# A mixture-of-experts layer on one core: the second lowest pick's rows come in by an adding DMA, the third lowest pick's during the loop, and the first products no longer stand behind the slot lists

## The reference, cut to what matters

```python
def _L0_ffn_ref(h, gate_w, gu_w, dp_w, sh_gate_w, sh_up_w, sh_down_w, sh_gate1_w):
    ...
    logits = x @ gate_w.T
    topv, topi = jax.lax.top_k(logits, TOP_K)
    rw = jax.nn.softmax(topv.astype(jnp.float32), axis=-1).astype(x.dtype)
    W = jnp.zeros((N, E), x.dtype).at[jnp.arange(N)[:, None], topi].set(rw)
    gu = jnp.einsum('nh,eih->nei', x, gu_w)
    gate, up = (gu[..., :I], gu[..., I:])
    inter = jax.nn.silu(gate) * up
    inter_w = inter * W[:, :, None]
    out = jnp.einsum('nei,ehi->nh', inter_w, dp_w)
    ...
    out = out + sh_g * sh_out
    return out.reshape(Bb, Tt, Hh)
x = L0_attn_X
...
h = _layernorm(x, axis=-1) * (1 + ca) + sa
x = x + ga * _L0_attn_ref(h, L0_attn_W_in, L0_attn_b_in, L0_attn_W_out, L0_attn_b_out)
h = _layernorm(x, axis=-1) * (1 + cb) + sb
x = x + gb * _L0_ffn_ref(h, L0_ffn_gate_w, ...)
return x
```

## Time and profile before

| | us |
|---|---|
| median of 3 runs (981.03 to 982.82) | 981.03 |
| the profiled execution's own time | 980.68 |
| its span, first to last instruction | 978.9 |
| the first two tiles' products | 378.7 to 389.0 |
| loop at its steady pace | 402.5 to about 897 |
| last result tile copied on DVE | 902.9 |
| first late read issued after the loop | 906.2 |
| last DVE step of the last group | 976.4 |

### The profile page before, as it was taken

How to read it: one execution, slowest core, us unless ns; L and a number is a source line. 1 busy time by engine, 2 the same in 40 slices (tenths; PEclk the granted TensorE clock), 3 DMA queues, 4 the chain that set the end, 5 groups by cost and what they waited for, 6 DMA issues and landing times.

```text
span 978.9 us, 18595 instructions
## 1 busy us (share of the span) xinstructions
PE 918.3 (94%) x3569; PEld 565.5 (58%) x3570; DVE 551.1 (56%) x1466; ACT 270.7 (28%) x789; POOL 465.7 (48%) x462
## 2 busy tenths in 40 slices
PE   6999999999999796799999999999999999997796
PEld 2434534444453543677777777777777777775342
DVE  3685776678767752344444444444444444444897
ACT  2012313123210301233333333333333333332000
POOL 0000035406615677466666657666656666666000
PEclk9999999999999699799999999999999999999799
DMA  9914003012102143477666778777778767897798
GB/s 341 327 69 151 1 0 102 1 44 76 28 0 69 46 146 92 154 237 245 232 232 229 257 250 278 271 242 241 237 234 274 248 235 235 297 400 287 278 420 341
DMA packets 68518, 192.06 MB, mean 196 GB/s; under 512 B 19926, under 2 KB 20438, under 8 KB 68104
## 3 DMA queue, kind: packets, MB, share of 16 engines
q1 hardware_dynamic: 38232, 120.28, 34.4%
q0 software_dynamic: 30256, 71.43, 22.2%
HBM read 158.98 MB, written 52.54 MB: 216 GB/s over the span
## 4 chain that ended last, share of the span: by engine, by line
PE 64%; DMA 8%; DVE 7%; POOL 6%; issue 6%; SPq 1%; DVEq 0%; POOLq 0%
PE bank L1612 25%; PE bank L1620 13%; PE bank L1385 7%; PE bank L1607 6%; POOL slot_table L566 5%; PE bank L1430 4%; DMA wqkv<-in_experts 3%; PE bank L1396 3%; DMA front<-y_rows 2%; PE bank L1627 2%; PE bank L1685 1%; DMA slot_table<-pair,place 1%; PE bank L1407 1%; DMA y_rows<-front,sid 1%; PE bank L1494 1%
## 5 line engine op out<-in xcount | busy, mean ns | idle before, releaser
L1612 PE MATMUL bank<-wqkv,h2T 128*128 x1280 | 306.2, 382 | 0.8 <-DMA wqkv<-in_experts 0.8
L566 POOL DMA_INDIRECT slot_table<-pair,place x128 | 129.7, 1013 | 250.2 <-DVE place L1003 187.5
L1612 PEld LDWEIGHTS bank<-wqkv,h2T 128*128 128x128 f32 x1280 | 232.9, 192 | 26.8 <-issue 1.3
L614 POOL DMA_INDIRECT y_rows<-front,sid x160 | 163.4, 1021 | 130.0 <-issue 68.4
L604 POOL DMA_INDIRECT front<-h_rows,gid x167 | 170.9, 1023 | 58.5 <-issue 44.0
L1620 PE MATMUL bank<-wqkv,front 128*128 x320 | 164.5, 596 | 1.4 <-DVE front L1290 1.4
L795 ACT ACTIVATE h2T<-bank 128x512 f32<-128x512 f32 x162 | 96.6, 597 | 202.5 <-PE bank L1607 202.5
L1290 DVE COPY front<-bank 128x128 f32<-128x128 f32 x160 | 46.7, 292 | 168.4 <-PE bank L1627 165.9
L1284 DVE COPY front<-bank 128x512 f32<-128x512 f32 x160 | 110.7, 692 | 43.3 <-PE bank L1620 43.0
L1607 PEld LDWEIGHTS bank<-const,front 128*128 128x128 f32 x648 | 81.2, 142 | 90.0 <-issue 85.3
L1385 PE MATMUL bank<-wqkv,front 128*128 128x512 f32 x256 | 115.6, 603 | 8.3 <-DVEq L935 6.2
(11 more groups left out here) (237 smaller groups left out, 757.7 us busy)
## 6 DMA issues: line engine op xcount, KB each, us to landing
wqkv<-in_experts SPq DMA_DIRECT2D x64, 768.0 KB
front<-y_rows SPq DMA_DIRECT2D x20, 768.0 KB, 9.5
wqkv<-y_rows SPq DMA_DIRECT2D x12, 768.0 KB, 13.1
front<-in_w_mod SPq DMA_DIRECT2D x5, 1024.0 KB, 10.2
x<-in_x SPq DMA_DIRECT2D x4, 1024.0 KB, 11.1
h_rows<-h SPq DMA_DIRECT2D x4, 1024.0 KB, 4.6
out_dram<-x SPq DMA_DIRECT2D x16, 256.0 KB, 10.2
wqkv<-in_w_in SPq DMA_DIRECT2D x3, 1024.0 KB, 13.7
```

The costliest lines, as they stand in the source:

```text
L566: pool.indirect_dma_start(out=slots[:, :], out_offset=bass.IndirectOffsetOnAxis(ap=place[b % 2][:, i, k:k + 1], axis=0), in_=pair[:, b * T ...
L614: pool.indirect_dma_start(out=y_rows[:, :], out_offset=bass.IndirectOffsetOnAxis(ap=sid[:, s:s + 1], axis=0), in_=yb[s % YBUFS], in_offset ...
L1612: mm = pe.matmul(bank[2 + s % 2][:, 0:GU], xT[s % 4][:, k, :], wqkv[:, bass.ds(w + k * GU, GU)], start=(k == 0), stop=(k == KC - 1))
```

## The change

Three things change.

1. **Products ahead of lists.** In the first round DVE no longer makes the lists of tiles 5, 6 and 7 (and waits for all table parts) before its first product. `gated(0)` is its first step; the lists of tiles 5 to 14 are made in later steps as the table `LISTS` says, one or two per step. The wait for table parts 3 to 5 now stands in step 3, ahead of the list of tile 7.
2. **Early and late picks.** Pick 7 is still read in the loop; in place of pick 6, pick 5 is (`read_early(2, 1, ...)`, which waits for expert 59 to have landed). Pick 6 is not read by SP at all: when POOL has issued everything of the loop, it issues 16 DMAs of 256 KB that add pick 6's rows onto pick 7's in `early[0]` (`accum_op=ALU.add`). They count up four semaphores `s_acc`, one for each four groups. DVE's 16 additions of L1317 go, and its second step of group g waits for the four additions of g's batch.
3. **Six groups of five late rows.** Five picks are read late: 0 to 2 (768 KB) and 3 to 4 (512 KB) by the two `read_back` of a group. There are six buffers (`BACK = 6`) in place of five, so the reads of group g+6 are issued when group g is finished. DVE's first step of a group adds pick 5 (`early[1]`) to pick 4.

```diff
--- before.py
+++ after.py
@@ -54,8 +54,10 @@
 ROUNDS = EXPERT_TILES // ROUND
 assert AHEAD <= ROUND == PLAN - EXPERT_TILES
 DUMMY_COL = EV * SLOT_COLS
-BACK = 5
-EARLY = 2
+BACK = 6
+EARLY = 3
+EARLY_ROWS = 2
+LOW = 3
 LATE = TOPK - EARLY
 BY_PE = 4
 NMOD = 6
@@ -203,17 +205,17 @@
         act, inter, iT = ([region[5][:, (2 * j + i) * P:(2 * j + i + 1) * P] for i in range(2)] for j in range(3))
         yb = [region[4][:, i * D:(i + 1) * D] for i in range(YBUFS)]
 
-        back_at = [((0, 1, 2), (9, 10, 11)), ((3, 4, 5), (12, 13, 14)), ((6, 7, 8), (23, 24, 25)),
-                   ((16, 17, 18), (26, 27, 28)), ((20, 21, 22), (29, 30, 31))]
-        back_half = [[(wqkv if h[0] >= 20 else front)[:, (h[0] % 20) * D:(h[0] % 20 + LATE // 2) * D]
-                      .rearrange("p (k d) -> p k d", k=LATE // 2) for h in halves] for halves in back_at]
-        back = [[half[:, k, :] for half in halves for k in range(LATE // 2)] for halves in back_half]
+        back_at = [((0, 3), (9, 2)), ((3, 3), (11, 2)), ((6, 3), (13, 2)),
+                   ((16, 3), (27, 2)), ((24, 3), (30, 2)), ((19, 3), (33, 2))]
+        back_half = [[(wqkv if at >= 24 else front)[:, (at % 24) * D:(at % 24 + n) * D].rearrange("p (k d) -> p k d", k=n)
+                      for at, n in halves] for halves in back_at]
+        back = [[half[:, k, :] for half, (at, n) in zip(*pair) for k in range(n)] for pair in zip(back_half, back_at)]
         early = ([wo[:, i, :] for i in range(4)] + [xn[:, i, :] for i in range(4)] + [h2[:, i, :] for i in range(4)]
                  + [rows_a[:, i, :] for i in range(3)] + [rows_b[:, i, :] for i in range(2)] + [bias_kv[:, i, :] for i in range(2)]
                  + [r[:, 2 * i:2 * i + 2, :].rearrange("p a c -> p (a c)") for r in (kcos, ksin) for i in range(2)]
                  + [qcos[:, :], qsin[:, :], shared_act[:, :], shared_inter[:, :]]
                  + [shared_w[:, i * D:(i + 1) * D] for i in range(3)] + [region[5][:, i * D:(i + 1) * D] for i in (2, 3)])
-        early = [early[k * TILES:(k + 1) * TILES] for k in range(EARLY)]
+        early = [early[k * TILES:(k + 1) * TILES] for k in range(EARLY_ROWS)]
         assert all(len(e) == TILES for e in early)
 
 
@@ -339,7 +341,7 @@
 
         s_fl = [[sem(f"s_fl{i}a"), sem(f"s_fl{i}b")] for i in range(BACK)]
         s_early = [sem(f"s_early{k}") for k in range(EARLY)]
-        s_esum = sem("s_esum")
+        s_acc = [sem(f"s_acc{i}") for i in range(TILES // TPB)]
         s_ft = sem("s_ft")
         s_fm = sem("s_fm")
         s_fo = sem("s_fo")
@@ -517,24 +519,30 @@
                     sp.wait_ge(landed, ((tiles + (YBUFS - 1 - j)) >> (YBUFS.bit_length() - 1)) * 16)
                     apart(sp)
 
-            def read_early(k, groups):
+            def read_early(k, row, groups):
                 all_landed(EXPERTS - (TOPK - 1 - k))
                 for g in groups:
-                    sp.dma_start(early[k][g], y_view[g, :, TOPK - 1 - k, :]).then_inc(s_early[k], 16)
+                    sp.dma_start(early[row][g], y_view[g, :, TOPK - 1 - k, :]).then_inc(s_early[k], 16)
 
             def read_back(g, h):
-                sp.dma_start(back_half[g % BACK][h], y_view[g, :, h * LATE // 2:(h + 1) * LATE // 2, :]).then_inc(s_fl[g % BACK][h], 16)
-
+                ks = (slice(0, LOW), slice(LOW, LATE))[h]
+                sp.dma_start(back_half[g % BACK][h], y_view[g, :, ks, :]).then_inc(s_fl[g % BACK][h], 16)
+
+            first_half, second_half = range(0, TILES // 2), range(TILES // 2, TILES)
             with sp.Fori(WSLOTS + 1, EXPERTS - 3) as e:
                 next_w(e)
-            for e in range(EXPERTS - 3, EV):
-                next_w(e)
-                n = e - (EXPERTS - 3)
-                read_early(n // 2, range(TILES // 2 * (n % 2), TILES // 2 * (n % 2 + 1)))
-            all_landed(EXPERTS - LATE // 2)
-            for g in range(3):
+            next_w(EXPERTS - 3)
+            read_early(0, 0, first_half)
+            next_w(EXPERTS - 2)
+            read_early(0, 0, second_half)
+            next_w(EXPERTS - 1)
+            read_early(2, 1, first_half)
+            next_w(EXPERTS)
+            read_early(2, 1, second_half)
+            all_landed(EXPERTS - LOW)
+            for g in range(4):
                 read_back(g, 1)
-            for g in range(3, BACK):
+            for g in range(4, BACK):
                 done = sp.value_load(cum_i[0:1, EXPERTS - BACK + g:EXPERTS - BACK + g + 1], min_val=1, max_val=EXPERT_TILES)
                 sp.wait_ge(s_d, done)
                 apart(sp)
@@ -649,6 +657,11 @@
                     round_pool(r)
             for n in range(AHEAD):
                 pool.wait_ge(s_xg[n], used * 16 + 16)
+            pool.wait_ge(s_early[0], 16 * TILES)
+            pool.wait_ge(s_early[2], 16 * TILES)
+            apart(pool)
+            for g in range(TILES):
+                pool.dma_start(early[0][g], y_view[g, :, TOPK - 2, :], accum_op=ALU.add).then_inc(s_acc[g // TPB], 16)
 
 
         @block.scalar
@@ -1264,7 +1277,6 @@
                     shared_inner(LAST)
                     shared_sum(HELD)
                     shared_sum(LAST)
-                    first_tokens(range(5, AHEAD))
                     ve.wait_ge(s_sht, TILES)
 
             def gated(t, s):
@@ -1289,18 +1301,31 @@
                     ve.wait_ge(s_d, t - 1)
                 ve.tensor_copy(iT[s % 2], bank[6 + s % 2][:, 0:P]).then_inc(s_iT, 1)
 
+            LISTS = [(), (5,), (6,), (7, 8), (9, 10), (11, 12), (13,), (14,)]
+
+            def first_lists(s):
+                for n in LISTS[s]:
+                    if n < AHEAD:
+                        first_tokens([n])
+                    else:
+                        if n == AHEAD:
+                            for i in range(3, len(PARTS)):
+                                ve.wait_ge(s_tbl[i], 16)
+                        tokens(n, n % ROUND)
+
             def round_ve(r):
                 for s in range(ROUND):
                     t = r * ROUND + s
-                    tokens(t + AHEAD, (s + AHEAD) % ROUND)
+                    if isinstance(r, int):
+                        first_lists(s)
+                    else:
+                        tokens(t + AHEAD, (s + AHEAD) % ROUND)
                     if not (isinstance(t, int) and t < 1):
                         take_inter(t - 1, (s - 1) % 2)
                     gated(t, s)
                     if not (isinstance(t, int) and t < 2):
                         take_y(t - 2, r if s >= 2 else r - 1, (s - 2) % ROUND)
 
-            for i in range(3, len(PARTS)):
-                ve.wait_ge(s_tbl[i], 16)
             round_ve(0)
             used = rounds_used(ve)
             with ve.Fori(1, ROUNDS) as r:
@@ -1311,16 +1336,13 @@
             take_y(used * ROUND - 1, used - 1, ROUND - 1)
 
 
-            for k in range(EARLY):
-                ve.wait_ge(s_early[k], 16 * TILES)
-            for g in range(TILES):
-                ve.tensor_tensor(early[0][g], early[0][g], early[1][g], ALU.add).then_inc(s_esum, 1)
+            ve.wait_ge(s_early[2], 16 * TILES)
             tf = Tally(s_fm)
             for g in range(TILES):
                 part = back[g % BACK]
                 ve.wait_ge(s_fl[g % BACK][1], 16 * (g // BACK + 1))
-                step(tf, ve.tensor_tensor(part[4], part[4], part[5], ALU.add))
-                ve.wait_ge(s_esum, g + 1)
+                step(tf, ve.tensor_tensor(part[4], part[4], early[1][g], ALU.add))
+                ve.wait_ge(s_acc[g // TPB], 16 * TPB)
                 step(tf, ve.tensor_tensor(part[4], part[4], early[0][g], ALU.add))
                 ve.wait_ge(s_ft, g + 1)
                 step(tf, ve.tensor_tensor(part[4], part[4], bank[g % BACK][:, :], ALU.add))
@@ -1680,8 +1702,8 @@
                 if g >= BACK:
                     pe.wait_ge(s_fo, g - BACK + 1)
                 for k in range(BY_PE):
-                    if k % (LATE // 2) == 0:
-                        pe.wait_ge(s_fl[g % BACK][k // (LATE // 2)], 16 * (g // BACK + 1))
+                    if k in (0, LOW):
+                        pe.wait_ge(s_fl[g % BACK][k // LOW], 16 * (g // BACK + 1))
                     mm = pe.matmul(bank[g % BACK][:, :], ident, back[g % BACK][k], start=(k == 0), stop=(k == BY_PE - 1))
                 mm.then_inc(s_ft, 1)
```

## The result

| | before | after |
|---|---|---|
| median | 980.86 (978.46 to 982.82, 10 runs) | 983.63 (980.76 to 986.96, 10 runs) |
| ratio, with its 95% interval | | 1.0035 [1.0019, 1.0051] |
| profiled execution, its span | 980.68, 978.9 | 983.68, 981.8 |
| last result copy ends | 902.94 | 897.27 |
| from there to the span's end (the tail) | 76.0 | 84.5 |

The changed kernel is slower by 0.35%, and the whole interval lies above 1. The forecast was 975.8, faster. The two halves of the forecast part here: the loop ends earlier, as forecast, and the tail is 8.5 longer where 2.8 was forecast.

The account below looks back on a forecast made before the run. PE was taken to bound the loop at 3.14 us a tile, and full DMA engines the tail's end. 981.03 - 8.0 (start) + 2.8 (tail) = 975.8 us; range 970.5 to 983.5, the forecast case's own 973 to 979.

Parts of the forecast that it names:

- Part 1, -8.0: Start of the loop: products ahead of lists let tile 5's products start earlier, -8.0 us, bounds 5.2 and 8.4.
- The tie to the list of tile 7: Start: the gather tile 5's products need hangs on this list, which waits for the table and does not move.
- Part 2a, SP in the loop, 0: Loop's end: early reads now need expert 59 in place of 58, whose rows land in time; cost 0.
- Part 2b, removing 16 additions gains nothing: Start of the tail: DVE's 16 additions are under cover of the late reads and PE's first group; gain 0.
- Part 2b, how the adds are issued: After POOL's last loop branch: 1.3 us an issue, all 16 from 905.8 to about 927, the first four by 911.
- the first read shares the engines with four additions: Start of the tail: sharing the DMA engines delays DVE's first group, +1.2 us.
- DVE floor: Tail if DVE paces it: 918.25 + 1.2 + 2.1 + 15 x 3.50 = 974.1, against 976.4 before.
- Parts 2c and 3, an add priced at 1.5 times a plain read: Tail: 2.9 MB more on full DMA engines, +7.0 us, less 4.2 for a filled dip, sum +2.8.
- The six buffers fill the dip of 918 to 925, -4.2: Tail: engines fell to 156 GB/s with five buffers full; six buffers and the additions fill this, 4.2 us.
- Additions cost two reads: Rival in the tail: an add takes 2 times a plain read, tail +7.8, total 980.8; chance 0.23.
- The slower rival: Tail, 907 to some 950: an add costs 3 times or more and holds up SP's reads, total 991; chance 0.11.
- a tail over 86: Last result copy to the end: above this the forecast sign, faster, would be wrong; 78.8 was forecast.

Follow-up runs that it names:

- e1: Kernel before with products ahead of lists alone, its tail untouched; 972.16 us, ratio 0.9921.
- e7: Kernel before with products ahead of lists and a sixth buffer for six late rows, no adds; 969.45 us, ratio 0.9891.
- e8: e1 with the lists of tiles 5 and 6 ahead of the first product again; 973.24 us, ratio 0.994.
- e4: Changed kernel, all 16 adds issued but no group before the last waits for them, pick 5 added twice; 984.55 us, ratio 1.0035.
- e3: Changed kernel with POOL's 16 adds made plain reads, same queue, moment and wait; 972.77 us, ratio 0.9923.
- e5: Changed kernel without the 16 adds and the wait for them, pick 6 left out; 969.11 us, ratio 0.9889.
- e6: Changed kernel with only the first 8 of the 16 adds, pick 6 left out for groups 8 to 15; 979.26 us, ratio 0.9994.
- e2: Changed kernel with the first round's lists in their old order, so the tail's change alone; 990.67 us, ratio 1.0101.

## Why the prediction was wrong, step by step

- **Part 1, -8.0: right.** Alone it measured -8.2. In e1's trace 7.5 of that is the earlier end of the loop; its tail is also 1.4 shorter than in the trace of before, which part 1 does not touch, so that the match to 0.2 is in part luck. PE's idle time and the half clock of the earlier trace rows are gone, and the loop's end was seen 7.8 earlier over ten traces. The forecast of tile 5's products at 401 was 3 off in the changed kernel's trace (404.01), because the table landed 3.1 later in it; in e1, where it landed 0.9 later than before, they start at 401.82. The tie to the list of tile 7, on which the step rested, is right: the idle time of 1.76 ends with a gather, and tile 5's products start 5.0 to 5.1 behind that list in the changed kernel, e1, e7 and e8, where 4.9 was forecast. The late table in the changed kernel's trace looks like chance, though that is not settled: the list of the first tile came at 364.4 there and in e4, and at 360.8 to 362.9 in e1, e3, e5, e6 and e7, which have the same start.
- **Part 2a, SP in the loop, 0: right.** The early reads were issued at 855.65, right behind the load at 853.81, with no wait for expert 59's rows.
- **Part 2b, removing 16 additions gains nothing: right.** e7 keeps them and has the shortest tail of all.
- **Part 2b, how the adds are issued: wrong.** I took 1.3 an issue from the indirect DMAs and so spread the 16 until 927. They are issued from 900.8 at 0.55 each, all by 909.1, while the first late reads are in the same engines. The first batch then landed at 920.5. This wait had no price beyond "the first read shares the engines with four additions (+ 1.2)". That price stood in the DVE floor alone. S grew by 8.7. On its own this costs 9.3 (e6, with 8 adds). With all 16 it is hidden: the other limit binds, by 3.5.
- **Parts 2c and 3, an add priced at 1.5 times a plain read: this is the step that failed.** I took the middle of 1 and 2 as no row was nearer. It measured 2.15 by the queues' shares, 2.1 by the tails. Put into the prediction's own arithmetic, +2.8 becomes +9.3 by extrapolating its two values (2.8 at 1.5, 7.8 at 2). The tail grew by 8.5 against the trace of before, by 9.9 against e1. The way of counting, engines' time up to the last group's read, was right, and the mis-sized term is the price of an add. By the Trainium skill (page "Collectives: The Full Stack", section "The bandwidth ceiling: the fold count and why AG ≠ RS ≠ AR") the adding step of a collective needs two source reads and so runs at half the rate, with 1.93 measured. This case's adds go the same way and cost somewhat more, 2.1 to 2.15. The prediction had this rule before it and took a middle that no row supported.
- **The six buffers fill the dip of 918 to 925, -4.2: right in kind, 3.3 in size (L of e1 against e7).** e7 has it by itself. In the changed kernel the adds had eaten it: the dip is there in GB/s (204) at a share of 1.13.
- **The rivals.** "Additions cost two reads" gave 980.8 and a tail of 83.8; measured 983.63 and 84.5. It was this one. The slower rival's threshold, 2.2 times, lay just beyond what the adds cost, and its place (907 to some 950) is where the engines move 204 to 319 GB/s. It had 0.11, and slower as a whole 0.13, although 2.15 lies between the two. Its price of 3 times is ruled out. The prediction's mark for a wrong sign, a tail over 86, was set too high: with 8.0 gained at the start the tail breaks even at 76.0 + 8.0 = 84.0, and it is 84.5.
- **The sum.** With part 1 at -8.2 and the tail at +8.5 it is 980.86 - 8.2 + 8.5 = 981.2; with the tail of e1 as its base, +9.9, it is 982.6; by the medians of e1 and e2, 980.86 - 8.2 + 10.3 = 983.0, against 983.63. The 10.3 of e2 is 1.8 more than the tails of e2 and before explain, and lies within the 8.5 to 10.8 that five traces of the old tail give. The range of 970.5 to 983.5 missed by 0.1. In the prediction's arithmetic its upper end is a price of about 2.3, and the measured 2.15 gives 982.3, inside it; the last 1.3 were in no term. That the miss is as small as this says nothing for the forecast, whose middle was 7.8 off and whose sign was wrong.

## What to carry to other kernels

An accumulating DMA takes work off an engine and costs the DMA engines, here, 2.15 times the time of a plain read. Look first at which of the two is full: here DVE had 4.36 to spare, and the DMA engines, but for a dip of 6.7, nothing, so the trade went the wrong way. Where DMA queues share full engines, price a transfer by the engines' time it takes, not by its bytes, and check both limits, the landing that the first consumer needs and the sum up to the end; removing the longest wait in a profile (e4) changes nothing while the second limit stands right behind it. Take a baseline from more than one trace: the tail of the kernel before moved by 2.3 between traces. A buffer more was the cheap remedy where the engines fell idle for lack of a free one (e7).
